# The sort's record in exact 16-bit pieces with paired columns, and the side work set at other steps

## Time and profile before

| | |
|---|---|
| median of the runs | 1304.96 us |
| profiled execution | 1306.58 us |
| its span, first to last instruction | 1304.7 us |
| mean granted TensorE clock | 0.943 of full |
| PE, PEld busy | 1135.4 us (87%), 1003.3 us (77%) |
| DVE, ACT, POOL busy | 852.6 (65%), 534.8 (41%), 615.7 us (47%) |
| before the loop over groups | 0 to 115 us |
| the loop | 115 to about 830 us |
| gate and experts | to 1304.7 us |

### The profile page before, as it was taken

The page is one execution under the profiler, slowest core; times in us unless marked ns, Lnnn a source line. Parts: engine busy times, 40 slices in busy tenths (PEclk is TensorE's granted clock), DMA queues, the critical chain, the costliest instruction groups (busy, mean ns, idle before and its releaser), DMA issues.

```text
span 1304.7 us, 21589 instructions
## 1 busy us (share of the span) xinstructions
PE 1135.4 (87%) x6735; PEld 1003.3 (77%) x6735; DVE 852.6 (65%) x1988; ACT 534.8 (41%) x1247; POOL 615.7 (47%) x623
## 2 busy tenths in 40 slices
PE   6997899998989999898998997752999999999980
PEld 5786687786867778687786876652999999999980
DVE  7866788888888898988888877945222222222226
ACT  4756666483755738466483742121111111011100
POOL 5856457566475655656566472001233333333320
PEclk9998899999999999999999999756999999999995
DMA  7223123222232222222222231116699999999949
GB/s 211 83 65 117 56 67 90 66 81 71 63 90 70 86 70 77 77 70 81 69 86 74 65 89 41 61 38 214 229 334 332 333 333 334 335 329 332 333 166 295
DMA packets 118414, 196.12 MB, mean 150 GB/s; under 512 B 13567, under 2 KB 67645, under 8 KB 118333
## 3 DMA queue, kind: packets, MB, share of 16 engines
q1 hardware_dynamic: 88998, 120.62, 27.8%
q0 software_dynamic: 26112, 71.34, 17.3%
q10 hardware_dynamic: 3222, 3.20, 0.7%
HBM read 177.12 MB, written 17.99 MB: 150 GB/s over the span
## 4 chain that ended last, share of the span: by engine, by line
PE 51%; DVE 21%; DVEq 11%; issue 9%; ACT 4%; DMA 2%; SPq 1%; ACTq 1%; POOL 0%; POOLq 0%
PE psum L981 18%; PE psum L991 8%; DVE agg L1226 5%; PE psum L905 5%; DVE agg L1232 4%; PE psum L915 3%; PE psum L724 3%; ACT in_slot L390 2%; PE psum L698 2%; PE psum L792 2%; DVE hot L1219 2%; PE psum L844 1%; DVEq L1311 1%; DVEq L1072 1%; DVEq L1088 1%
## 5 line engine op out<-in xcount | busy, mean ns | idle before, releaser
L642 POOL DMA_INDIRECT arena<-y_rows,gather_i x416 | 443.9, 1067 | 288.7 <-PE psum L905 139.9
L905 PE MATMUL psum<-arena,hot 128*128 128x256 f32 x832 | 222.7, 398 | 14.3 <-DVE hot L1219 6.2
L1226 DVE TENSOR_TENSOR agg<-psum,agg 128x256 f32 x416 | 174.1, 419 | 45.2 <-DVE agg L1226 21.3
L487 ACT ACTIVATE arena<-arena,listed 128x256 f32<-128x256 f32 x416 | 175.0, 495 | 70.0 <-DMA arena<-y_rows,gather_i 69.9
L905 PEld LDWEIGHTS psum<-arena,hot 128*128 128x128 f32 x832 | 153.0, 196 | 50.2 <-issue 23.1
L981 PEld LDWEIGHTS psum<-arena 128*128 128x128 f32 x1536 | 181.7, 195 | 4.9 <-issue 2.5
L981 PE MATMUL psum<-arena 128*128 128x128 f32 x1536 | 182.1, 278 | 1.9 <-DVE arena L1564 1.9
L1571 DVE TENSOR_TENSOR arena<-psum,arena 128x512 f32<-128x512 f32 x64 | 44.3, 692 | 205.1 <-PE psum L981 205.1
L577 ACT ACTIVATE arena<-psum 128x512 f32<-128x512 f32 x64 | 38.2, 597 | 328.1 <-PE psum L981 328.1
L658 POOL DMA_INDIRECT chosen_rows<-arena,back_at x64 | 63.2, 987 | 220.3 <-DVE arena L1578 215.5
L915 PE MATMUL psum<-arena,hot 128*128 x624 | 151.1, 383 | 1.8 <-DVE agg L1232 0.6
(11 more groups left out here) (212 smaller groups left out, 1622.2 us busy)
## 6 DMA issues: line engine op xcount, KB each, us to landing
arena<-in_L_ffn_w_dram SPq DMA_DIRECT2D x144, 512.0 KB, 5.6
xnT<-in_L_ffn_w_dram SPq DMA_DIRECT2D x48, 512.0 KB, 5.6
arena<-y_rows,gather_i POOLq DMA_INDIRECT x416, 2.8
arena<-chosen_rows SPq DMA_DIRECT2D x8, 640.0 KB, 8.9
y_rows<-w ACTq DMA_DIRECT2D x6, 512.0 KB, 2.9
agg<-in_x_dram SPq DMA_DIRECT2D x4, 640.0 KB, 6.8
n_rows<-arena SPq DMA_DIRECT2D x4, 640.0 KB
out_dram<-agg SPq DMA_DIRECT2D x4, 640.0 KB
```

The costliest lines, as they stand in the source:

```text
L487: last = act.activation(rows[h][:, t, :], rows[h][:, t, :], ACT.Copy, scale=weight[h][:, t:t + 1])
L642: pool.indirect_dma_start(rows[h][:, t, :], None, y_rows, bass.IndirectOffsetOnAxis(ap=gather_i[h][:, t:t + 1], axis=0)).then_inc(gathered ...
L905: pe.matmul(bank_of(g, t // 2)[:, (t % 2) * C:(t % 2 + 1) * C], hot[:, n % HOTS, :], rows[h][:, t, :], start=True, stop=True).then_inc(met, 1)
L1226: dve.tensor_tensor(own, bank_of(g, t // 2)[:, (t % 2) * C:(t % 2 + 1) * C], own, ALU.add).then_inc(evicted, 1)
```

## The change

The record is made in bfloat16 in seven fields in place of three in float32. Source and destination are split each into a multiple of 64 and the rest below 64, and the weight into three bfloat16 pieces that add up to it; each piece is exact. Edges stand in pairs of columns, so that the innermost step of all operands is 1, and one product on VectorE makes the whole record of a chunk. The marks of bins, of tiles and of slots are bfloat16 too. TensorE reorders 224 columns in one pass in place of 96 in two. After the reordering, VectorE adds the pieces. Before the loop the pieces are made from the loaded edges. The steps of the side work are set anew on all three engines. The diff, cut to its core:

```diff
-    FIELDS = 3
+    FIELDS = 7
+    LOW = 64
...
-        in_bin = sb("in_bin", [P, BINS, GE])
+        pieces = sb("pieces", [P, COLS // 2, FIELDS, 2], BF16)
+        piece = [pieces[:, :, f, :] for f in range(FIELDS)]
+        in_bin = sb("in_bin", [P, BINS, GE], BF16)
...
-        record = [sb(f"record{k}", [P, CH, FIELDS, GT]) for k in range(2)]
-        in_slot = [sb(f"in_slot{k}", [P, CH, P]) for k in range(2)]
+        record = [sb(f"record{k}", [P, CH // 2, FIELDS, GT, 2], BF16) for k in range(2)]
+        in_slot = [sb(f"in_slot{k}", [P, CH, P], BF16) for k in range(2)]
...
@@ ScalarE, the loop over g: the order for g >= 1 after the change
+                    message_turned(g), scale_rows(g, 7), std(0, g), keep_list(g + 1), n1_turned(g)
+                    scale_rows(g + 1, 0), hidden_relu(g, 0), scale_rows(g + 1, 1)
+                    slot_hot(g + 2, 0), slot_hot(g + 2, 1), hidden_relu(g, 1), scale_rows(g + 1, 2)
+                    slot_hot(g + 2, 2), scale_rows(g + 1, 3), query_exp(g + 1), std(1, g)
+                    scale_rows(g + 1, 4), slot_hot(g + 2, 3), scale_rows(g + 1, 5), scale_rows(g + 1, 6)
@@ TensorE
-                    last = pe.matmul(in_order, in_slot[k % 2][:, c, :], record[k % 2][:, c, :, :].rearrange("p f t -> p (f t)"),
+                    last = pe.matmul(in_order, in_slot[k % 2][:, c, :], record[k % 2][:, c // 2, :, :, c % 2].rearrange("p f t -> p (f t)"),
@@ TensorE beside(g, step), g >= 1: step before, step after
-  turn_tok(msg) 2, merge 5, turn_list 5, pick_list 8, turn_tok(n1) 14, hidden 21 23 25 26, prefix 22, query 29
+  turn_tok(msg) 3, merge 6, turn_list 11, pick_list 15, turn_tok(n1) 15, hidden 19 23 26 33, prefix 21, query 27
-  reorder 34 46 48 55, down 38 43, attend 49
+  reorder 36 45 52 53, down 38 41, attend 50
@@ VectorE
             def mark_tiles(g, k):
+                whole = [P, CH // 2, GT, 2]
+                two = place_b[:, own].rearrange("p (a b) -> p a b", b=2)
+                dve.tensor_tensor(in_tile[:, :, :, :], two.unsqueeze(2).to_broadcast(whole), tile_of[:, :, :].unsqueeze(1).to_broadcast(whole),
+                                  ALU.is_equal)
-            def make_field(g, k, f):
+            def make_record(g, k):
+                dve.drain()
+                if g * CHUNKS + k >= 2:
+                    dve.wait_ge(reordered, g * CHUNKS + k - 1)
+                first = (g * GE + k * CH) // 2
+                own = pieces[:, first:first + CH // 2, :, :].rearrange("p a f b -> p (a f) b")
+                tiles = in_tile[:, :, :, :].rearrange("p a t b -> p a (t b)")
+                dve.tensor_tensor(record[k % 2][:, :, :, :, :].rearrange("p a f t b -> p a f (t b)"),
+                                  tiles.unsqueeze(2).to_broadcast([P, CH // 2, FIELDS, 2 * GT]),
+                                  own.unsqueeze(2).to_broadcast([P, CH // 2 * FIELDS, GT, 2]), ALU.mult).then_inc(record_ready, 1)
@@ read_list and place_list
-                dve.tensor_copy(gather_i[h][:, :], in_order[:, GT:2 * GT])
-                dve.tensor_copy(listed[h][:, :, :], in_order.rearrange("p (f t) -> p f t", f=FIELDS)[:, 0:3:2, :])
+                dve.tensor_copy(parts[:, :, :], part[:, 1:FIELDS:2, :])
+                dve.drain()
+                dve.tensor_tensor(node[h], part[:, 0, :], parts[:, 0, :], ALU.add)
+                dve.tensor_tensor(gather_i[h][:, :], part[:, 2, :], parts[:, 1, :], ALU.add)
+                dve.tensor_tensor(weight[h], part[:, 4, :], parts[:, 2, :], ALU.add)
...
+                dve.tensor_tensor(weight[h], in_order[:, 6 * GT:7 * GT], weight[h], ALU.add)
@@ split_places
+                dve.tensor_copy(place_b[:, :], place_i[:, 1, :])
@@ before the loop, VectorE, 128 x 416 each
-            dve.tensor_copy(edge[:, 0, :], edge_i[:, 0, :])
-            dve.tensor_copy(edge[:, 1, :], edge_i[:, 1, :])
+            dve.tensor_copy(piece[4], weight_in[:, :].rearrange("p (a b) -> p a b", b=2))
+            for end in range(2):
+                dve.tensor_scalar(edge_part[:, 0, :], edge_i[:, 1 - end, :], LOW * (LOW - 1), None, ALU.bitwise_and)
+                dve.tensor_scalar(edge_part[:, 1, :], edge_i[:, 1 - end, :], LOW - 1, None, ALU.bitwise_and)
+                dve.drain()
+                dve.tensor_copy(piece[2 - 2 * end], edge_part[:, 0, :].rearrange("p (a b) -> p a b", b=2))
+                dve.tensor_copy(piece[3 - 2 * end], edge_part[:, 1, :].rearrange("p (a b) -> p a b", b=2))
+                dve.drain()
...
+            for k in range(2):
+                subtract piece[4 + k] from weight_in, drain, copy to piece[5 + k], drain
@@ VectorE beside(g, step), g >= 1: step before, step after
-  keep_picked 12, mark_bins 14, count_marks 15, add_prefix 18, mask 19, sum 20, split 21
+  keep_picked 11, mark_bins 13, count_marks 14, add_prefix 18, mask 19, sum 20, split 21
-  mark_tiles 22 28 33 44, make_field 23 24 27 / 29 30 32 / 36 39 43 / 46 48 49
+  mark_tiles 23 28 31 39, make_record 26 30 37 49
-  bins_named 38, pair_stats 44, pair_moments 45, centre 45 46, add_dense 47 49
+  bins_named 35, pair_stats 42, pair_moments 44, centre 45 48, add_dense 49 50
-  message_sums 50, message 52 54, read_list 53, place_list 55
+  message_sums 51, message 52 53, read_list 52, place_list 55
```

More of the change, by code:

```diff
@@ L522, in _ @@
                     slot_hot(g + 2, 0)
-                hidden_relu(g, 0)
+                    slot_hot(g + 2, 1)
+                hidden_relu(g, 1)
                 if more:
@@ L526, in _ @@
                 if sorts:
-                    slot_hot(g + 2, 1)
-                hidden_relu(g, 1)
+                    slot_hot(g + 2, 2)
                 if more:
@@ L868, in beside @@
                     hidden(g, 1)
-                if step == 25:
+                if step == 26:
                     hidden(g, 2)
-                if step == 26:
+                if step == 27 and more:
+                    query(g + 1)
+                if step == 33:
                     hidden(g, 3)
-                if step == 29 and more:
-                    query(g + 1)
-                if step == 34 and sorts:
+                if step == 36 and sorts:
                     reorder(g + 2, 0)
@@ L1354, in beside @@
                         message(0, step - 5)
+                if g >= 1 and step == 0 and more:
+                    clip_starts(g + 1)
+                if g >= 1 and step == 2 and more:
+                    drop_whole(g + 1)
+                if g >= 1 and step == 3 and more:
+                    mark_starts(g + 1)
                 if step == (13 if g == 0 else 4):
@@ new lines, in beside @@
+                if step == 11 and more:
+                    keep_picked(g + 1)
+                if step == 13 and sorts:
+                    mark_bins(g + 2)
+                if step == 14 and sorts:
+                    count_marks(g + 2)
+                if step == 18 and sorts:
+                    add_prefix(g + 2)
+                if step == 19 and sorts:
+                    mask_places(g + 2)
+                if step == 20 and sorts:
+                    sum_places(g + 2)
+                if step == 21 and sorts:
+                    split_places(g + 2)
@@ new lines, in beside @@
+                if step == 23 and sorts:
+                    mark_tiles(g + 2, 0)
+                if step == 26 and sorts:
+                    make_record(g + 2, 0)
+                if step == 28 and sorts:
+                    mark_tiles(g + 2, 1)
+                if step == 30 and sorts:
+                    make_record(g + 2, 1)
+                if step == 31 and sorts:
+                    mark_tiles(g + 2, 2)
+                if step == 37 and sorts:
+                    make_record(g + 2, 2)
@@ L1373, in beside @@
                     centre(g, 1)
-                if step == 47:
+                if step == 49 and sorts:
+                    make_record(g + 2, 3)
+                if step == 49:
                     add_dense(g, 0)
-                if step == 49:
+                if step == 50:
                     add_dense(g, 1)
-                if step == 50 and more:
+                if step == 51 and more:
                     message_sums(g + 1)
+                if step == 52 and sorts:
+                    read_list(g + 2)
@@ L1380, in beside @@
                 if step == 52 and more:
                     message(g + 1, 0)
-                if step == 54 and more:
+                if step == 53 and more:
                     message(g + 1, 1)
+                if step == 55 and sorts:
+                    place_list(g + 2)
             def add_up(g, its_bin):
```

150 lines of the change are left out of this document (62 added, 88 removed).

## The result

| | before | after |
|---|---|---|
| median of the runs beside each other | 1304.59 us (1303.73 to 1305.18, 4 runs) | 1287.02 us (1286.79 to 1288.07, 4 runs) |
| ratio, 95% interval | | 0.9865 (0.9852 to 0.9878) |
| profiled execution, its span | 1306.58, 1304.7 us | 1286.79, 1285.0 us |

A forecast was written before the change was run, and what follows sets the result against it. The prediction took VectorE's own sequence as the beat, with TensorE close behind. Loop -24 us and preamble +2 gave -22 on 1306.6: 1284.6, or 1283 for the median of runs, range 1268 to 1303.

The forecast's parts named there:

- VectorE's sequence is the beat: Loop: DVE's own sequence sets the 56.3 us beat, PE close behind; a free PE would give back under 1 us.
- some 10 us of slack: TensorE in the loop: after the change PE has some 10 us of slack in a beat of 54.
- A 55.3 group becomes 54.0: Quiet groups of the loop: DVE's changed operations and steps sum to -1.3 us, bounds -2.2 and -0.3.
- the load's 0.9: Register load moved from step 38 to 35, partly under the hot batch: gain 0.9 us per group (0.2 to 1.1).
- The slow groups lose 3.3 each: Five 57.3 us groups: their extra 2.0 us is PE's and falls into PE's new slack: -3.3 each.
- Group 0, -1.3: First group of the loop: has its own start and counts with -1.3 us.
- Groups 11 and 12, 0: Last two groups of the loop: they sort nothing and keep their work, so 0.
- The start, +2: Before the loop: eleven more DVE operations cost 9 us, partly given back; net +2 us (-1 to +5).
- A: Rival on DVE's 16-bit products: one element a cycle, +4.9 us per group, about 1338 us; chance 0.07.
- B: Rival on ACT: its chain ends after DVE's step 51, about 1302 to 1308 us; chance 0.07.
- C: Rival on the clock: 1.2 GHz stretches stay or grow, costing 2 us in five groups, 1293 us; chance 0.2.
- D: Rival: DVE gives back more, load wholly hidden, records under 1.0 us, preamble at 0: 1272 us; chance 0.16.

The follow-up runs named there:

- 4: Changed kernel with five small float32 products adding zeros in each reordering chunk on TensorE: 1287.2 us, 0.9857 of the kernel before.
- 3: Kernel before with every second product of the reordering left out, so half of each list is missing: 1296.84 us, 0.9921 of the kernel before.
- 5: Changed kernel with one more unread 128 x 256 float32 product on VectorE behind each record: 1303.83 us, 0.9981 of the kernel before.
- 8: Kernel before with only hidden_relu(g, 0) moved ahead of the first slot_hot on ScalarE: 1288.3 us, 0.9869 of the kernel before.
- 6: Changed kernel with the register load back at step 38 in place of 35: 1296.15 us, 0.9927 of the kernel before.
- 1: Kernel before with the 16-bit record but all side work at the old steps: 1300.46 us, 0.9963 of the kernel before.
- 12: Float32 record with the new steps, and group 0's picks and prefix(2) placed as in experiment 11: 1286.67 us, 0.986 of the kernel before.
- 11: Changed kernel with group 0's old picks, two groups' pieces cut first, and prefix(2) at TensorE's step 17 in group 0: 1280.81 us, 0.9808.
- 9: Changed kernel with turn_list, pick_list and keep_picked of group 0 at their old steps: 1282.96 us, 0.9829 of the kernel before.
- experiment 2: Old float32 record with the new steps on the three engines: 1288.76 us, 0.9887 of the kernel before.
- 10: Changed kernel with group 0's picks at the old steps and the pieces of two groups cut first, the others later: 1281.4 us, 0.9817.
- 7: Changed kernel with hidden_relu(g, 0) back behind scale_rows and the first slot_hot on ScalarE: 1343.77 us, 1.0294 of the kernel before.

## Why the prediction came out

The sum held (-22 forecast, -19.8 in the profiled executions); of its two main mechanisms one held, and the other was for the larger part put down to the wrong part of the change. That the total came so near is partly luck: g1 to g11 gave 3.8 us more than forecast (26.8 for 23), and the start and group 0 took 5.7 more (+6.4 for +0.7).

- **VectorE's sequence is the beat:** right. More work on PE costs nothing (4), less work on PE doesn't shorten a quiet beat by more than some 0.2 us (3), more work on VectorE costs all of its spacing (5). The "under 1 us" that a free PE could give back fits too: moving the relu gave some 0.6 (8). But "some 10 us of slack" for PE doesn't follow from the rows: 23.04 + 27.69 us busy less 3.8 is 46.9, 7 us in a beat of 54. Over g1 to g10 PE is not busy for 6.4 us a group, under the 8 that I had named as a sign of being right.
- **A 55.3 group becomes 54.0:** 53.75 on average, inside the bounds. The durations of the new operations were right within some 5%, the load's 0.9 was 0.8 (6). The record alone took 0.3 off the quiet groups (1), where I had expected 0.4. The -1.3 has another make-up than mine, though: in the kernel before, some 0.6 came with relu_h's wait (8), which I had priced at "perhaps the last 0.3". What the remaining moves of steps cost wasn't measured one by one.
- **The slow groups lose 3.3 each:** right in size (56.9 to 57.7 became 53.6 to 54.2), wrong in cause for the larger part. I wrote that their 2.0 us "is PE's and falls into PE's new slack". The slack takes only about half of it: a slow group stays 1.0 us longer than a quiet one with half of the reordering (3) and 0.7 with the 16-bit record (1), against 1.9 before, and the falls of the clock stay. One moved relu removes them with PE at its full work (8). Of the 25.4 us of g1 to g10, the relu's place is 16.2 (562.9 to 546.7), the other steps 3.0 (to 543.7), the record 6.2 (to 537.5). The shares hang on the order in which the parts are added: the record is worth 9.7 alone (562.9 to 553.2 in experiment 1) and 3.8 between experiments 12 and 11. And the other steps' 3.0 is a balance, since the load's place alone is worth 7.8 of it in the changed kernel (6). I had seen the 2.63 us wait, the fall behind it, and that the wait goes; I didn't join them.
- **Group 0, -1.3:** the term that failed outright. Group 0 got 3.0 longer. I counted it like the others, but merge stands at step 12 there, and pick_list is now behind it at 15, while VectorE wants the picks at 11. I had asked what a moved step is queued behind for g >= 1 alone. That cost 4.5 us (9); without it the group comes out near the forecast.
- **Groups 11 and 12, 0:** group 11 lost 1.4. The new steps bring it, not the record, the relu or the load: it takes 43.5 us in experiment 2 and 43.7 in 6, but 45.3 in 1 and 45.1 in 8.
- **The start, +2:** 3.4. The 15 operations took 12.3 us against 2.9, +9.4 for 9 forecast; so less came back than I took. VectorE's timeline after, from the first of them to the first marks of bins:

```profile
31.01 0.37 DVE L1197 CAST pieces<-weight_in 128x416 bf16<-128x416 f32 x1
31.29 0.90 DVE L1199 TENSOR_SCALAR edge_part<-edge_i 128x416 int32<-128x416 int32 x1
...
43.32 0.94 DVE L1057 TENSOR_TENSOR in_bin<-bin_b,bin_no 128x800 bf16<-128x800 bf16 x1
```

  Executions scatter: group 0 begins at 114.9 to 119.1 us in the five kernels with the float32 record and at 120.6 to 123.2 in the seven with the uncut preparation. Cutting only the first pieces gives 1 to 2.5 us back (10, 11).
- **Rivals.** A is refuted by 1102 ns. B by VectorE's timeline, where step 52's first operation stands without a wait:

```profile
401.34 0.25 DVE L1287 RECIPROCAL tiny<-tiny 128x16 f32<-128x16 f32 x1
401.67 0.26 DVE L1127 COPY parts<-psum 128x96 f32<-128x96 f32 x1
```

  B's own time is mis-summed: with the quiet groups' gain gone and the slow groups' 2.0 us still saved, it comes to some 1299 us, not 1302 to 1308, and the high end of the range was set with it. C: the clock in g1 to g10 is 1.00. But C named the right thing, a gap at PE, and 7 shows the price of a gap at the query, wait and half clock together: some 56 us over the changed kernel. D didn't come: a record takes 1.10 us and the load still adds some 0.5. Behind the row of C stood the Trainium skill, "TensorE: Matmul & The Clock Gate", section "HAM oscillation"; 7 and 8 agree with it that pauses between bursts of products bring the fall. That the amount of TensorE's work doesn't is what 3, 4 and 8 show. The rate rule of the Trainium skill, "VectorE: DVE Perf Modes", section "The perf-mode tier table", agrees also where the repeated operand has four dimensions: 1792 elements in 1102 ns.

Open: why the same wait of 2.63 to 2.98 us brings a half-clock stretch in only five of ten groups of the kernel before, and what makes group 0 longer than the others by 6 us even in experiment 11. In 11 the tile half of group 0 gained 4.2 us and the span only 0.4: the crossing half lost 1.4, the start 1.3 and g1 to g10 1.1. Why wasn't followed.

## What to carry to other kernels

If an engine's idle gap and a fall of the clock stand next to each other in the trace, move what the gap waits for before anything else: one call on ScalarE was worth 18 us here, and less work on TensorE left the falls in place and only halved their cost. Price a moved step in each group that has its own order, the first above all. And test a large change by halves: alone they gained 5 and 15 to 17 us, together 18, and the larger part of that was one call.

## What the runs showed of the hardware

- A wait of some 5.6 us on TensorE went with half clock in ten groups of ten (7); one of 2.6 to 3.0 us in five of ten (kernel before), six (3) and four (1). One of 1.87 us went with it in two groups of ten (1). In the changed kernel and experiments 2, 4, 5, 6 and 8 to 12, where no single wait in g1 to g10 is over 1.9 us, one group of a hundred had a half-clock stretch (11).
- Less work on TensorE doesn't stop such a fall but takes in part of it: a group with one is longer by 1.9 us in the kernel before, by 1.0 with half of the reordering (3) and by 0.7 with the 16-bit record (1).
- A product on VectorE over 4 x 7 x 32 x 2 elements in 16 bits, both inputs repeated by a step of 0 and the innermost step 1, runs at 0.615 ns an element with its fixed part. With four more 256-element float32 products the beat grew by 0.38 us each, though each is busy for 0.43 (5).
- Loading 32 registers on VectorE takes 2.10 us of its queue wherever it stands, and it starts while the operation before it is running. With a hot batch of 1.2 us and an eviction beside it, it adds some 0.5 us to the beat; with a record of 1.1 us alone, some 1.3 (6).
